# A routed two-branch layer: router by four column strips, turned back by TensorE, roots of eight tiles at a time, zeros behind expert 0's rows

## What is computed

```python
xn = layernorm(x)
x = x + attn(xn) + ffn(xn)

def ffn(x):                                  # t = 4096 tokens, E = 8, cap = t / E = 512
    probs = softmax(xf @ Wr)                 # the router
    eidx = argmax(probs)
    p_tok = probs[eidx]
    onehot = one_hot(eidx, E)
    rank = (cumsum(onehot) - onehot)[eidx]   # how many tokens before it chose this expert
    keep = rank < cap
    xe = xf[dispatch]                        # rows of each expert, by expert and rank
    ye = relu(xe @ W1[e]) @ W2[e]
    y[dispatch] += ye * p_tok * keep
```

## Time and profile before

| | us |
|---|---|
| median of 3 runs | 130.85 (130.85 to 131.13) |
| span of the profiled execution | 128.8 |
| around the span (median less span) | 2.05 |
| TensorE busy | 106.2 |
| VectorE busy | 101.8 |
| ScalarE busy | 99.6 |
| GpSimd busy | 84.6 |

### The profile page before, as it was taken

How to read it: one execution, slowest core, us unless ns; L and a number is a source line. 1 busy time by engine, 2 the same in 40 slices (tenths; PEclk the granted TensorE clock), 3 DMA queues, 4 the chain that set the end, 5 groups by cost and what they waited for, 6 DMA issues and landing times.

```text
span 128.8 us, 2229 instructions
## 1 busy us (share of the span) xinstructions
PE 106.2 (82%) x711; PEld 89.9 (70%) x711; DVE 101.8 (79%) x238; ACT 99.6 (77%) x219; POOL 84.6 (66%) x109
## 2 busy tenths in 40 slices
PE   3999999999799999999999997999997999700000
PEld 3999976672379779789879987898697899600000
DVE  5398998999699999979614489999999975973690
ACT  3299792888589589789689999999999799823560
POOL 8987774078788787778777877888787878700000
PEclk9999999999999999999999999999999999998555
DMA  2966964892456365312611711111110111149995
GB/s 85 383 247 173 405 244 173 318 380 66 103 169 181 80 209 139 118 53 56 209 41 41 219 51 41 61 37 41 52 57 25 60 43 61 41 108 302 325 372 215
DMA packets 8234, 19.27 MB, mean 150 GB/s; under 512 B 1689, under 2 KB 1945, under 8 KB 8224
## 3 DMA queue, kind: packets, MB, share of 16 engines
q1 hardware_dynamic: 5424, 13.70, 31.5%
q0 software_dynamic: 2080, 4.19, 11.2%
q10 hardware_dynamic: 720, 1.25, 2.6%
HBM read 10.82 MB, written 8.39 MB: 149 GB/s over the span
## 4 chain that ended last, share of the span: by engine, by line
PE 60%; DVE 9%; DMA 8%; ACT 8%; issue 5%; POOL 4%; POOLq 1%; SPq 1%; DVEq 0%; ACTq 0%
PE bank L624 17%; PE bank L609 6%; PE bank L611 6%; PE bank L610 6%; DMA dec<-y_rows 4%; PE bank L640 4%; PE bank L453 3%; PE bank L561 3%; PE bank L442 3%; POOL xn_tok L405 3%; DMA xn_tok<-xn_rows,idx_in 2%; ACT xc L796 2%; PE bank L594 2%; PE bank L563 2%; PE bank L562 2%
## 5 line engine op out<-in xcount | busy, mean ns | idle before, releaser
L405 POOL DMA_INDIRECT xn_tok<-xn_rows,idx_in x32 | 33.7, 1054 | 14.4 <-issue 9.4
L417 POOL DMA_INDIRECT y_rows<-xn_tok,idx_out x32 | 33.5, 1047 | 9.7 <-issue 9.1
L624 PE MATMUL bank<-w_raw,h_sb 128*128 128x128 f32 x256 | 29.9, 275 | 0.0
L624 PEld LDWEIGHTS bank<-w_raw,h_sb 128*128 128x128 f32 x256 | 29.2, 192 | 0.0
L786 ACT ACTIVATE h_sb<-bank 128x512 f32<-128x512 f32 x32 | 18.8, 598 | 2.5 <-PE bank L611 0.6
L609 PE MATMUL bank<-xg_hi,w_hi 128*128 128x512 f32 x32 | 13.2, 412 | 0.0
L611 PE MATMUL bank<-xg_hi,w_lo 128*128 128x512 f32 x32 | 12.6, 393 | 0.0
L610 PE MATMUL bank<-xg_lo,w_hi 128*128 128x512 f32 x32 | 12.5, 391 | 0.0
L1021 DVE SCALAR_TENSOR_TENSOR xc<-xnT,par,xc 128x1020 f32<-128x1020 f32 (+2 forms) x9 | 11.5, 1277 | 0.3
L640 PE MATMUL bank<-par,xc 128*128 128x128 f32 x64 | 8.8, 280 | 2.2 <-ACT xc L796 1.3
L1061 DVE TENSOR_TENSOR_SCAN xnT<-dec,bank 128x256 f32<-128x256 f32 x16 | 10.1, 674 | 0.3
(11 more groups left out here) (143 smaller groups left out, 243.2 us busy)
## 6 DMA issues: line engine op xcount, KB each, us to landing
w_raw<-in_weights SPq DMA_DIRECT2D x8, 512.0 KB, 3.9
y_rows<-sca SPq DMA_DIRECT2D x4, 512.0 KB, 5.9
dec<-y_rows SPq DMA_DIRECT2D x8, 256.0 KB, 5.7
x_tok<-in_x SPq DMA_DIRECT2D x3, 512.0 KB, 5.9
xn_rows<-xn_tok SPq DMA_DIRECT2D x3, 512.0 KB, 3.6
out<-dec SPq DMA_DIRECT2D x4, 256.0 KB, 3.1
out<-dec ACTq DMA_DIRECT2D x4, 256.0 KB, 2.9
x_tok<-in_x SPq DMA_DIRECT2D x2, 256.0 KB, 3.5
```

The lines of the kernel that those rows point to most:

```text
L405: g.indirect_dma_start(gathered[:, s * D:(s + 1) * D], None, xn_rows, bass.IndirectOffsetOnAxis(ap=idx_in[:, s:s + 1], axis=0)).then_inc(g ...
L417: g.indirect_dma_start(y_rows, bass.IndirectOffsetOnAxis(ap=idx_out[:, s:s + 1], axis=0), gathered[:, s * D:(s + 1) * D], None, bounds_che ...
L624: last = mm(tile_of(e, s), h_sb[:, k * CAP + s * P:k * CAP + (s + 1) * P], w_raw[:, e, F + k * D:F + (k + 1) * D], start=(k == 0), stop=(k ...
```

## The change

The router's weights become stationary, 32 columns wide, and 512 tokens move; four calls write four strips of 32 partitions of one bank, ScalarE copies the bank (`keep_logits`), and TensorE turns it back by four transposes (`by_token`). Roots and reciprocals are taken for eight tiles at a time; the shift is computed by GpSimd. ScalarE normalises 10 tiles and GpSimd 22. The constant `values` is filled by three engines. moments(4) stands before marks(0). TensorE's order is new: `counts(0)` behind both routers, table matmuls in five parts between column groups. `totals` goes through ScalarE. SyncE's zeros wait for expert 0's rows. Cut to its core:

```diff
+STRIP = 32
-        w_router = sb("w_router", [P, P])
+        w_router = sb("w_router", [P, STRIP])
+        count16 = sb("count16", [P, P], F16)
+        logitsT = [xc[:, 0:HT], xc[:, HT:2 * HT]]
-        logits = [bank[6][:, 0:PT * E], bank[2][:, 0:PT * E]]
-        table = bank[3][:, 0:NS]
-        before = [bank[7][:, 0:E * PT], bank[6][:, 2 * E * PT:3 * E * PT]]
+        strips = [bank[6], bank[2]]
+        table = bank[7][:, 0:NS]
+        before = [bank[3][:, 0:E * PT], bank[3][:, E * PT:2 * E * PT]]
+        ACT_TILES = (3, 7, 11, 15, 19, 22, 23, 27, 30, 31)
+        POOL_TILES = tuple(t for t in range(NT) if t not in ACT_TILES)
...
             sp.wait_ge(zeroed, 1)
+            sp.wait_ge(gather_in[0], 16 * ST)
...
+            g.iota(values[:, 0:QUARTER, :], ...)            # GpSimd: one quarter of values, not four
+            def inverse(q):
+                pool.wait_ge(stat_done, (q + 1) * QT // 2)
+                g.tensor_scalar(nmr[:, cols], stats[:, cols, 1], -1.0, None, ALU.mult)
+                pool.wait_ge(rstd_done, q + 1)
+                g.tensor_tensor(nmr[:, cols], nmr[:, cols], rstd[:, cols], ALU.mult)
+            for q in range(NQ):
+                inverse(q)
+                normalise(q)
...
-            for _ in range(7):
+            for _ in range(5):
                 mm(bank[7][:, 0:P], ident[:, :], ident[:, :], start=True, stop=True)
+            def router(h):
+                if h == 0:
                     pe.wait_ge(router_w, 1)
+                transposed(pe, 4 * h + 3)
+                for j in range(P // STRIP):
+                    n = 4 * h + j
+                    last = mm(strips[h][j * STRIP:(j + 1) * STRIP, :], w_router[:, :], xT[:, n * HT:(n + 1) * HT],
+                              start=True, stop=True, tile_position=(0, j * STRIP))
+                last.then_inc(strips_done, 1)
+            def by_token(h):
+                pe.wait_ge(logitsT_done, h + 1)
+                for i in range(4):
+                    last = nc.tensor.transpose(strips[h][:, i * P:(i + 1) * P],
+                                               logitsT[h][:, i * P:(i + 1) * P], ident[:, :])
                 last.then_inc(logits_done, 1)
...
+            turned(0)
+            (centred)
+            for n in range(1, 5):
+                turned(n)
+            router(0)
+            turned(5)
+            by_token(0)
+            turned(6)
             columns_of(0)
+            turned(7)
+            columns_of(1)
+            router(1)
+            counts(0)
+            columns_of(2)
+            by_token(1)
+            columns_of(3)
             conv(0, 0, 2)
             counts(1)
+            (counted)
+            conv(0, 2, 3)
             table_of(0)
+            table_of(8)
+            columns_of(4)
             conv(0, 3, TAPS)
+            columns_of(5)
+            table_of(16)
+            columns_of(6)
+            table_of(22)
+            columns_of(7)
+            table_of(28)
             conv(1, 0, TAPS)
...
+            (ScalarE)
+            for part in (1, 2):                              # two quarters of values, from count16
+                a(values[:, v0:v1, :], count16[...], ACT.Copy).then_inc(valued, 1)
+            untile(0), untile(1), root(0), untile(2), untile(3), root(1), untile(4), keep_logits(0), untile(5),
+            normalise(0), normalise(1), root(2), untile(6), untile(7), root(3), keep_columns(0), normalise(2),
+            keep_logits(1), normalise(3), keep_columns(1), normalise(4), normalise(5), keep_columns(2)
+            act.wait_ge(counted_done, 1)
+            a(totals[:, :], counted, ACT.Copy).then_inc(totals_done, 1)
             normalise(6)
             normalise(7)
+            keep_columns(3)
...
+            (VectorE; its quarter of values stands ahead)
+            moments(0), moments(1), (w_router), moments(2), inverse(0), moments(3), inverse(1), moments(4), inverse(2)
             marks(0)
             inverse(3)
-            moments(4)
             ranks(0)
-            inverse(4)
             places(0)
+            lows(0)
             marks(1)
+            lows(8)
             ranks(1)
             places(1)
+            lows(16), lows(22), lows(28)
```

More of the change, by code:

```diff
@@ L474, in counts, with table_of @@
                    stop=True).then_inc(before_done, 1)
[L476 to L481, removed]
+            def table_of(t0):
+                t1 = (LOW_STARTS + (NT,))[LOW_STARTS.index(t0) + 1]
+                pe.wait_ge(hi_done, t0 // PT + 1)
+                pe.wait_ge(low_done, LOW_STARTS.index(t0) + 1)
+                if t0 == 0:
+                    pe.wait_ge(totals_done, 1)
+                for t in range(t0, t1):
+                    last = mm(table, low_eq[:, :, t],
+                              hi_val[:, t // PT, :, :, t % PT].rearrange("p e s -> p (e s)"),
                               start=(t == 0), stop=(t == NT - 1))
-                if h == NP - 1:
+                if t1 == NT:
                     last.then_inc(table_done, 1)
@@ L497, in columns_of @@
                 last.then_inc(xn_tp, 1)
[L499 to L517, removed]
-            columns_of(0)
-            router(NH - 1)
+            turned(0)
+            pe.wait_ge(par_in, 16)
+            pe.wait_ge(centre_done, 1)
+            mm(centred, centre[:, :], par[:, ROUTER:ROUTER + STRIP], start=True, stop=True).then_inc(centre_mm, 1)
+            for n in range(1, 5):
[4 more added lines that the diff above has]
+            turned(6)
+            columns_of(0)
+            turned(7)
[5 more added lines that the diff above has]
+            columns_of(3)
             def conv(n, first, last_tap):
@@ L574, in _ @@
             for h in range(NP):
-                last = mm(totals, ones[:, :], run[:, h, :, PT - 1], start=(h == 0), stop=(h == NP - 1))
-            last.then_inc(before_done, 1)
+                last = mm(counted, ones[:, :], run[:, h, :, PT - 1], start=(h == 0), stop=(h == NP - 1))
+            last.then_inc(counted_done, 1)
+            conv(0, 2, 3)
             table_of(0)
-            columns_of(3)
-            conv(0, 2, 3)
-            table_of(1)
+            table_of(8)
+            columns_of(4)
             conv(0, 3, TAPS)
-            for n in range(4, NH):
-                columns_of(n)
+            columns_of(5)
[4 more added lines that the diff above has]
+            table_of(28)
             conv(1, 0, TAPS)
@@ L675, in _, with root @@
             nc.scalar.preload_act_table_set("sqrt_and_others")
[L677 to L679 removed]
+            def root(q):
+                cols = slice(q * QT, (q + 1) * QT)
+                if q == 0:
                     act.wait_ge(eps_done, 3)
[L681 to L683 removed]
+                act.wait_ge(stat_done, (q + 1) * QT // 2)
+                a(std[:, cols], stats[:, cols, 2], ACT.Sqrt, bias=eps[:, 0:1], scale=1.0 / D).then_inc(std_done, 1)
             def normalise(n):
[L686 removed]
+                act.wait_ge(nmr_done, n // 2 + 1)
                 for t in range(4 * n, 4 * n + 4):
@@ L896, in _ @@
             v.tensor_scalar(half_b[:, :], par[:, BIAS_R:BIAS_I + 1], 0.5, None, ALU.mult).then_inc(coef, 1)
+            moments(2)
+            inverse(0)
+            moments(3)
+            inverse(1)
+            moments(4)
             inverse(2)
-            moments(3)
             results = [0]
@@ L910, in per_token, with by_group, by_group_of @@
                 return ap.unsqueeze(2).to_broadcast([P, n, E])
-            lg = [part.rearrange("p (t e) -> p t e", e=E) for part in logits]
+            def by_group(ap):
+                return ap.rearrange("p (j i) -> p j i", i=RUN)
+            def by_group_of(ap):
+                return ap.rearrange("p (j i) e -> p j i e", i=RUN)
+            lg = [part[:, :].rearrange("p (i j w) -> p j i w", i=RUN, w=STRIP)[:, :, :, 0:E] for part in strips]
             number = [0] * NP
```

154 lines of the change are left out of this document (84 added, 70 removed).

## The result

The changed kernel takes 132.96 us (median of 4 runs, 132.70 to 133.67) against 130.85 (4 runs, 129.75 to 131.13): ratio 1.018, 95% interval 1.013 to 1.023: slower, clear of the noise, while the interval leaves open whether by 2% or less. The prediction was 133.3 (130.3 to 136.0). The direction, the size and one large term held; two other terms were wrong and partly cancelled.

A forecast was written before the change was run, and what follows sets the result against it. GpSimd's stream of 64 indirect DMAs was taken to bound the kernel, TensorE second with 1.7 us to spare. The stream's start, set by idx_in, moves +2.4 us, added to 130.85: 133.3 us, range 130.3 to 136.0.

The forecast's parts named there:

- Start of the phase, to marks(0): First router half starts at 8.6; VectorE's inverse(2) waits for root(2); marks(0) at 13.15 against 11.83, a new 1 us wait.
- rival A: The router's four strips run side by side, 0.86 us per half; idx_in at 25.1, 130.9 us, no gain; chance 0.36.
- Router: On TensorE, only the second instruction of one call overlaps the first of the next: 2.15 us per half.
- To run(1): From marks(0) on, counts(0) waits behind the second router half until 16.7; run(1) ends at 20.8, +0.1 us.
- From run(1) to idx_in: TensorE does counts, taps, tables and column groups in order, making this stretch 6.65 us against 4.43: +2.2 us.
- Sum: All steps up to idx_in together: it is ready at 27.5 against 25.1, +2.4 us.
- At nothing: Filling `values` and normalising on ScalarE and GpSimd cost nothing; the last normalised copy lands 1.2 us before idx_in.
- rival C: Copies of normalised rows come last as GpSimd's tiles slow: 1.5 us late (132.2) under rival A; 0.06 together with rival D.
- Zeros behind expert 0's rows: Moved zero stores delay decay(0) at most 2 us and end before the first scatter matters; hidden, 0.3 us for TensorE.
- PE's 1.7 us: TensorE's time to spare behind GpSimd's DMA stream, taken from the last scatters coming 1.7 to 2.9 us after their data.
- rival D: Zeros slow expert 1's gathers to 6 from 3.3 us; TensorE loses 2.6, 0.3 + 1.5 spare: +0.8; 0.06 with rival C.

The follow-up runs named there:

- both moves taken back: Changed kernel with column groups 4 to 7 behind the last table matmul again and the zeros right behind the normalised rows again: 130.10 us, ratio 0.9946 against the kernel before.

## Why the prediction was right and wrong

*Start of the phase, to marks(0):* 13.15 predicted, 12.80 measured, for another reason. VectorE's inverse(2) did wait for root(2), 1.05 us, as written. But router(0) took 1.06 us and not 2.15, and it started at 9.40 and not 8.6, as x landed later (the first matmuls on the fourth load at 8.81). Where it started at 8.64, in the run with split calls, marks(0) came at 12.07, near rival A's 11.85.

*Router: wrong.* The step that failed is "the two instructions of a call use the same strip, so the second can't run before the first is through, and all rows show matmuls starting in program order". The first half stands; the second does not hold between strips. The first instructions of all four calls start within 20 ns of each other at 9.40, the second ones 0.45 later, and a half takes 1.06 us. Column strips side by side, as "TensorE: Matmul & The Clock Gate" of the Trainium skill has them in Part 3, is what the trace shows: 1.06 us for four calls that take 3.44 one after another, 3.2 times. The same section's strict program order does not hold here between strips, and I had built the forecast on it. All matmul rows of before used all columns of the array, so they could say nothing on this; it was a rule taken beyond its rows. This was rival A's mechanism, given 0.36.

*To run(1):* 20.8 predicted, over at 20.00. The second half was no longer late, counts(0) came at 15.04.

*From run(1) to idx_in: right.* 6.65 predicted, 6.57 measured (20.00 to 26.57), with TensorE busy for 6.51 of it and the pieces in the order and at the prices given: 0.95 and 0.85 for the taps, 1.10 and three pieces for the tables, 0.44 per column group. With the columns behind the last table it was 5.15, in that run and in the one with both moves taken back.

*Sum:* idx_in at 27.5 predicted, 26.57 measured; +1.5 and not +2.4, and +0.4 in the execution where x landed sooner (25.47; rival A had said 25.1).

*At nothing:* the copies of normalised rows had 1.2 us to spare in the forecast, and in the changed kernel they did not end last. With idx_in earlier they did (25.51), as rival C says. Fills and normalising cost nothing that shows, but no run took them back alone.

*Zeros behind expert 0's rows: wrong, and the larger miss.* The step reads "both are inside PE's 1.7 us". It counted decay(0) and the first scatter, which were not late by themselves, and put what the zeros do to gathers in flight into rival D, at 0.06 together with C and +0.8 us. Measured: +1.3 in the changed kernel, +3.5 in the kernel before, where the stream grew from 85.46 to 89.40. The gather needed 6.65 and 6.86 us where D had said 6, near enough. What was off is the slack: D set 0.3 + 1.5 us against the delay. But the 1.7 was read at the end of the stream, at the last four scatters, and the slack at turn(1) was never read. Two timelines of the kernel before have it, GpSimd's issue of expert 1's last gather and TensorE's turn(1):

```profile
35.19 0.94 POOL L405 DMA_INDIRECT xn_tok<-xn_rows,idx_in  x1 [0.30 <-issue]
```

```profile
39.08 0.60 PE L594 MATMUL bank<-ident,xn_tok 128*128 128x128 f32 x4
```

No wait stands there, but the rows come just in time: this gather landed after 3.3 us, at 38.5, 0.6 before they are needed. A landing after 6.86 is 3.6 us later, and 3.2 of it became a wait. What followed made it worse in that run: the clock fell behind the wait, which neither D nor any other rival had.

So 133.3 against 132.96 is partly luck. In the profiled execution the start came 0.9 sooner than forecast, the stream was 2.1 longer and the tail 0.5 shorter; that makes 134.0, and the median is lower because the usual execution loses less than this one.

*Slips in the forecast itself.* Its chance for "slower" is given as 0.65, but the terms named for it add up to 0.73. Rival C's 132.2 does not follow from its 1.5 us, which give 132.4. Neither changes the number or the range.

## What to carry to other kernels

A transfer moved "out of the way" of one consumer has a new neighbour: look up which small gather shares the DMA engines with it in its new window, and read the slack at the consumer of that gather, not at the end of the kernel. Work put between the members of a chain that ends an engine's wait costs nearly its full length (1.4 of 4 x 0.44 us here by the traces, 1.7 by the times), however useful it is later. A wait that a late transfer makes can cost twice: look at the granted clock behind it as well. A matmul that fills only a quarter of the array's columns leaves the other three for calls on other strips, so the router of 8 outputs cost 1.06 us a half and not 3.44; the gain counts only where the router was in the way.

## What the runs showed of the hardware

- f32 matmuls on four column strips of 32 ran side by side, though the list has each strip's instructions together: 1.06 us for 8 instructions of 512 columns, 1.09 for 16 of 256.
- Four stores of 512 KB and a weight load brought the DMA share to 0.97 for 8 us, and a gather of 128 rows in their midst took 6.9 us to land instead of 3.3; with two of the stores 5.5.
- TensorE's granted clock fell to the lower level behind 2.32, 2.91, 2.98 and 3.22 us without work in four executions and stayed at 1.00 behind 2.16, 2.31 and 2.86 in three others; in one more it was at 0.50 from 22 to 28 us while TensorE was busy. Ahead of a landing it cost nothing that shows; ahead of 32 matmuls whose result a scatter waits for, it made these 5.37 us long instead of 3.74.
- The landing of the first loads differs by near 1 us between executions of nearly the same program (the first router half at 9.40, at 8.64 and at 8.31), which is as much as several of the edits here are worth.
